# Last halves transposed on TensorE, a new tail of the joint stage, and two steps moved in loops

## What is computed

```python
# L0: two wide attentions (16 heads of 64), then a gated feed-forward
h = layer_norm(x, ln1_g, ln1_b); x = x + attention(h, h, Wq1, Wk1, Wv1, Wo1, bo1)
h = layer_norm(x, ln2_g, ln2_b); x = x + attention(h, ctx, Wq2, Wk2, Wv2, Wo2, bo2)
x = x + gated_feed_forward(layer_norm(x, ln3_g, ln3_b))
# L1: a narrow attention (16 heads of 8) on ctx, then norm and feed-forward
out = narrow_attention(x, ctx); out = out + feed_forward(layer_norm(out)); x = x + out
# L2: wide attention (16 heads of 64) of layer_norm(x) on ctx
x = x + wide_attention(layer_norm(x), ctx)
# L3: narrow attention (16 heads of 8) of x on ctx
x = x + narrow_attention(x, ctx)
```

## Time and profile before

| | us |
|---|---|
| median of 3 runs | 1729.83 (1729.8 to 1731.36) |
| the profiled execution | 1727.86 |
| its span, first to last instruction | 1726.1 |

### The profile page before, as it was taken

One profiled execution on the slowest core, in us unless ns is written; L12 is line 12 of the kernel. 1 busy time (PEld: TensorE's weight loads), 2 busy tenths in 40 slices (PEclk: granted clock), 3 DMA queues, 4 the chain that ended last, 5 costly groups with the idle time before them and its releaser, 6 DMA issues. The chain is left out here.

```text
span 1726.1 us, 48944 instructions
## 1 busy us (share of the span) xinstructions
PE 1638.1 (95%) x16520; PEld 1351.9 (78%) x16520; DVE 1310.8 (76%) x2408; ACT 1240.9 (72%) x3858; POOL 677.3 (39%) x946
## 2 busy tenths in 40 slices
PE   7999999999999999989899998988999999999997
PEld 6888888888888888779777777867787888787875
DVE  5777777777777777747688887656888888888885
ACT  5777777777777777623388886456888888888885
POOL 3444444454444444413222222643343434343431
PEclk9999999999999999989999999999999999999999
DMA  7776777777767767730000000014434344343441
GB/s 198 198 189 185 190 194 187 219 208 205 194 184 190 186 188 185 209 86 1 1 2 0 0 0 1 0 38 135 137 118 134 118 127 124 121 131 119 133 131 53
DMA packets 230743, 216.51 MB, mean 125 GB/s; under 512 B 19874, under 2 KB 228324, under 8 KB 230628
## 3 DMA queue, kind: packets, MB, share of 16 engines
q1 hardware_dynamic: 230628, 215.17, 45.2%
HBM read 112.34 MB, written 102.76 MB: 125 GB/s over the span
## 5 line engine op out<-in xcount | busy, mean ns | idle before, releaser
L658 ACT ACTIVATE L_probs<-L_scores,L_neg_max 128x128 f32<-128x128 f32 x512 | 182.7, 386 | 134.6 <-DVE L_neg_max L740 134.6
L854 POOL TENSOR_TENSOR L_probs<-L_probs,L_inv_sum 128x1024 f32<-128x1024 f32 x128 | 242.8, 1897 | 88.4 <-DVE L_inv_sum L760 88.4
L734 DVE TENSOR_REDUCE L_row_max<-L_scores 128x8 f32<-128x1024 f32 x128 | 156.1, 1219 | 41.5 <-PE L_scores L534 41.5
L1957 POOL TENSOR_TENSOR L2L_w_probs<-L2L_w_probs,L2L_w_inv_sum 128x1024 f32<-128x1024 f32 x64 | 121.4, 1897 | 129.7 <-DVE L2L_w_inv_sum L1783 129.5
L766 DVE STREAM_TRANSPOSE L_squares<-L_probs 128x1024 f32<-128x1024 f32 x128 | 156.6, 1223 | 0.3 <-POOL L_probs L854 0.3
L581 PE MATMUL L_ring<-L_probsT,L_v 128*64 128x128 f32 x2048 | 127.9, 277 | 9.5 <-issue 8.6
L581 PEld LDWEIGHTS L_ring<-L_probsT,L_v 128*64 128x64 f32 x2048 | 111.2, 137 | 29.9 <-issue 27.0
L534 PE MATMUL L_scores<-L_kT,L_qT 64*128 64x128 f32 x2048 | 131.8, 278 | 0.9 <-ACT L_kT L647 0.9
L534 PEld LDWEIGHTS L_scores<-L_kT,L_qT 64*128 64x128 f32 x2048 | 119.4, 188 | 12.5 <-ACT L_oT L647 8.1
L750 DVE TENSOR_REDUCE L_sums<-L_probs 128x8 f32<-128x1024 f32 x64 | 78.1, 1220 | 66.1 <-ACT L_probs L665 66.1
L1581 ACT ACTIVATE L2L_w_probs<-L2L_scores,L2L_w_neg_max 128x128 f32<-128x128 f32 x256 | 90.5, 372 | 39.3 <-DVE L2L_w_neg_max L1747 39.3
(11 more groups left out here) (220 smaller groups left out, 4617.0 us busy)
## 6 DMA issues: line engine op xcount, KB each, us to landing
L_relay<-L_squares SPq DMA_DIRECT2D x128, 512.0 KB, 3.4
L_probsT<-L_relay SPq DMA_DIRECT2D x512, 128.0 KB, 3.6
L2L_relay<-L2L_w_squares SPq DMA_DIRECT2D x64, 512.0 KB, 3.4
L2L_w_probsT<-L2L_relay SPq DMA_DIRECT2D x256, 128.0 KB, 2.9
out_x<-x SPq DMA_DIRECT2D x32, 64.0 KB, 2.7
L0a_wq<-in_L_xattn_Wq SPq DMA_DIRECT2D x2, 256.0 KB, 3.1
L0a_wk<-in_L_xattn_Wk SPq DMA_DIRECT2D x2, 256.0 KB, 3.7
L0a_wv<-in_L_xattn_Wv SPq DMA_DIRECT2D x1, 512.0 KB, 6.5
```

The costliest lines, as they stand in the source:

```text
L658: done = nc.scalar.activation(slot_probs(at, 0)[:, n, :], scores[:, 0, r, i, :], ACT.Exp, scale=layer_of(at).scale, bias=neg_max[:, n:n + ...
L734: nc.vector.tensor_reduce(row_max[:, s, :], slot(s), AX.X, ALU.max).then_inc(max_ready[s], 1)
L854: nc.gpsimd.tensor_tensor(to, to, inv_sum[:, :, s, :].unsqueeze(3) .to_broadcast([TOKENS, 2, GROUP, TOKENS]), ALU.mult).then_inc(divided, 1)
L1957: nc.gpsimd.tensor_tensor(to, to, w_inv_sum[:, :, s, :].unsqueeze(3) .to_broadcast([TOKENS, 2, GROUP, TOKENS]), ALU.mult).then_inc(w_divid ...
```

## The change

Four parts, all in the order of the work; the arithmetic is the same.

1. **L0's last halves.** The probabilities of (item, half) (62,1), (63,0) and (63,1) are transposed by TensorE (eight transpositions a half, two ring banks, one copied out by ScalarE and one by VectorE) and take no squares and no DMA. L3's weights are turned one step earlier. On SyncE's queue, from step 59 on, `back` of half 1 is issued before `away` of the next item's half 0.
2. **L1.** T0 (four heads) of t is transposed ahead of `score(t+1)`; T1 stays behind it.
3. **Joint stage, every step.** n.hT moves behind q1: TensorE does q1, n.hT, k1; ScalarE copies q1, n.hT, k1 behind the first four narrow exponentials, where n.hT had been ahead of them. The ring order is changed to match.
4. **Joint stage, end.** Item 31's halves are transposed by TensorE (16 transpositions, four copies by ScalarE) in a step of its own (31), in which `w_weigh(31)` and w.Wo(31) follow too; `tail_step` has them no more. For that, sums and division of item 31's half 1 are moved ahead into step 30: VectorE's `w_add_up(31)` stands before `n_row_maxima` there, and GpSimd's `w_divide(31, 1)` before `n_add_bias`.

```diff
@@ wide_attention
-    weights_step = items - 1
+    weights_step = items - 2
+    by_pe = ((items - 2, 1), (items - 1, 0), (items - 1, 1))
-    other_orders[weights_step] = [("weights", 0, "dve")] + order
+    other_orders[items - 3] = order[:9] + [("T2", 1, "dve"), ("T3", 1, "act")] + order[9:]
+    other_orders[items - 2] = order + [("T0", 1, "act"), ("T1", 1, "dve"), ("weights", 0, "dve")]
+    other_orders[items - 1] = order[:9] + [("T2", 0, "dve"), ("T3", 0, "act")] + order[9:]
@@ sync
-                if here(At(t), 1):
+                second = here(At(t), 1) and (t + 1, 1) not in by_pe
+                next_first = here(At(t), 2) and (t + 2, 0) not in by_pe
+                if second:
                     away(At(t + 1), 1)
-                if here(At(t), 2):
+                if second and t >= items - 5:
+                    back(At(t + 1), 1)
+                if next_first:
                     away(At(t + 2), 0)
...
@@ tensor
                 if here(t, 0):
                     weigh(t, 0)
+                    if t.n == items - 3 and t.i is None:
+                        transpose_probs(t.plus(1), 1)
+                    if t.n == items - 1:
+                        transpose_probs(t, 1)
                     weigh(t, 1)
+                if t.n == items - 2:
+                    transpose_probs(t.plus(1), 0)
+                    turn_weights(t)
...
@@ narrow_attention, tensor
             def step(t):
+                if here(t, 0):
+                    transpose_probs(t, 0)
                 if here(t, 1):
                     score(t.plus(1))
                 if here(t, 0):
-                    transpose_probs(t, 0)
                     transpose_probs(t, 1)
@@ wide_and_narrow
-             ("n.iT", -3, "act"), ("n.hT", -1, "act"), ("w.q1", 2, "act"), ("w.k1", 2, "act"), ("n.PV", -3, "dve"),
+             ("n.iT", -3, "act"), ("w.q1", 2, "act"), ("n.hT", -1, "act"), ("w.k1", 2, "act"), ("n.PV", -3, "dve"),
...
@@ tensor
+            def last_wide_step(t):
+                w_transpose_probs(t, 0)
+                w_weigh(t.plus(-1), 0)
+                w_weigh(t.plus(-1), 1)
+                w_transpose_probs(t, 1)
+                n_transpose_probs(t.plus(-3), 0)
+                n_transpose_probs(t.plus(-3), 1)
+                w_project_out(t.plus(-1))
+                n_score(t.plus(-2))
+                n_transpose_probs(t.plus(-3), 2)
+                n_transpose_probs(t.plus(-3), 3)
+                n_transpose_inverses(t.plus(-3))
+                w_weigh(t, 0)
+                w_weigh(t, 1)
+                n_transpose_h(t.plus(-1))
+                n_weigh(t.plus(-3))
+                n_queries_keys(t.plus(-1))
+                w_project_out(t)
+                n_project_out(t.plus(-3))
+                n_values(t.plus(-2))
+
...
+                if here(t, 2):
+                    w_queries(t.plus(2), 1)
                 if here(t, -1):
                     n_transpose_h(t.plus(-1))
                 if here(t, 2):
-                    w_queries_keys(t.plus(2), 1)
+                    w_keys(t.plus(2), 1)
...
@@ scalar
-                if here(t, -1):
-                    n_turned_h(t.plus(-1))
                 if here(t, -2):
                     n_exponentiate_0(t.plus(-2), 0)
                 if here(t, 2):
-                    w_projections(t.plus(2), 1)
+                    w_projection(t.plus(2), "w.q1", w_qT, 1)
+                if here(t, -1):
+                    n_turned_h(t.plus(-1))
+                if here(t, 2):
+                    w_projection(t.plus(2), "w.k1", w_kT, 1)
...
@@ vector
                 if here(t, -1):
                     w_finish(t.plus(-1))
+                if t.n + 1 == LAST_WIDE:
+                    w_add_up(t.plus(1))
+                    w_invert(t.plus(1), 1)
                 if here(t, -2):
                     n_row_maxima(t.plus(-2), 0)
                     n_negate_maxima(t.plus(-2))
...
@@ gpsimd
                 if here(t, -1):
                     n_copy_rows(t.plus(-1))
+                if t.n + 1 == LAST_WIDE:
+                    w_divide(t.plus(1), 1)
+                if here(t, -1):
                     n_add_bias(t.plus(-1))
```

More of the change, by code:

```diff
@@ L585, in weigh, with transpose_probs @@
                 filled_by(last, f"PV{s}")
+            def transpose_probs(at, s):
+                pe.wait_ge(divided, at.times(2, s + 1))
+                for n in (2 * s, 2 * s + 1):
+                    to = start_fill(f"T{n}", at)
+                    for i in range(GROUP):
+                        last = nc.tensor.transpose(to[:, TOKENS * i:TOKENS * (i + 1)],
+                                                   slot_probs(at, s)[:, GROUP * (n % 2) + i, :], ident[:, :])
+                    filled_by(last, f"T{n}")
             def transpose_h(at):
@@ L789, in turned_weights, with turned_probs @@
                 done.then_inc(emptied["dve"], 1)
+            def turned_probs(at, n):
+                await_filled(dve, f"T{n}", at)
+                nc.vector.tensor_copy(turned_to(at, n), by_head(bank(f"T{n}", at))).then_inc(emptied["dve"], 1)
             def step(t):
@@ L799, in step @@
                     subtract_maxima(t.plus(2))
-                if t.n == weights_step:
-                    turned_weights(t)
                 if here(t, -1):
                     finish(t.plus(-1))
-                if here(t, 1):
+                if t.n == items - 3 and t.i is None:
+                    turned_probs(t.plus(1), 2)
+                if t.n == items - 2:
+                    turned_probs(t.plus(1), 1)
+                    turned_weights(t)
+                if t.n == items - 1:
+                    turned_probs(t, 2)
+                if here(t, 1) and (t.i is not None or (t.n + 1, 1) not in by_pe):
                     turn_squares(t.plus(1), 1)
@@ L814, in step @@
                     invert(t.plus(2), 1)
+                if here(t, 2) and (t.i is not None or (t.n + 2, 0) not in by_pe):
                     turn_squares(t.plus(2), 0)
@@ L1226, in wide_and_narrow @@
     LANDED = 16 * SQUARES
-    ring = Ring(order, range(first, last + 1), BATCHES, {t: tail_order for t in range(BATCHES, last + 1)})
+    ring = Ring(order, range(first, last + 1), BATCHES,
+                {LAST_WIDE: last_wide_order, **{t: tail_order for t in range(BATCHES, last + 1)}})
     chunks = INNER // 128
@@ L1498, in n_project_out, with w_transpose_probs @@
                                            start=True, stop=True), "n.Wo")
+            def w_transpose_probs(at, s):
+                pe.wait_ge(w_divided[s], at.times(1, 1))
+                for n in (2 * s, 2 * s + 1):
+                    to = start_fill(f"w.T{n}", at)
+                    for i in range(GROUP):
+                        last = nc.tensor.transpose(to[:, TOKENS * i:TOKENS * (i + 1)],
+                                                   w_slot(at, s)[:, GROUP * (n % 2) + i, :], ident[:, :])
+                    filled_by(last, f"w.T{n}")
+            def last_wide_step(t):
[18 more added lines that the diff above has]
+                n_values(t.plus(-2))
             def tail_step(t):
@@ L1833, in n_finish, with last_wide_step @@
                                         ALU.add).then_inc(emptied["dve"], 1)
+            def last_wide_step(t):
+                n_add_up(t.plus(-3))
+                n_invert(t.plus(-3), 1)
+                n_repeat_inverses(t.plus(-3))
+                w_finish(t.plus(-1))
+                n_row_maxima(t.plus(-2), 0)
+                n_negate_maxima(t.plus(-2))
+                n_row_maxima(t.plus(-2), 1)
+                n_weighted(t.plus(-3))
+                n_subtract_maxima(t.plus(-2))
+                w_finish(t)
+                n_finish(t.plus(-3))
+                n_invert(t.plus(-2), 0)
             def tail_step(t):
@@ L1841, in tail_step @@
                     n_negate_maxima(t.plus(-2))
-                if here(t, -1):
-                    w_finish(t.plus(-1))
                 if here(t, -2):
@@ L1880, in step @@
                     n_negate_maxima(t.plus(-2))
-                if here(t, 1):
+                if here(t, 1) and t.n + 1 != LAST_WIDE:
                     w_turn_squares(t.plus(1), 0)
@@ L1960, in step @@
             def step(t):
-                if here(t, 0):
+                if here(t, 0) and t.n != LAST_WIDE:
                     w_divide(t, 1)
```

105 lines of the change are left out of this document (78 added, 27 removed).

## The result

| | before | after |
|---|---|---|
| median of 4 runs each, us | 1729.82 (1729.15 to 1731.36) | 1746.54 (1746.21 to 1747.27) |
| the profiled execution | 1727.86 | 1747.27 |
| its span | 1726.1 | 1745.2 |
| TensorE matmul, busy | 1638.1 (95%) | 1659.5 (95%) |

The account below looks back on a forecast made before the run. TensorE, busy 95% of the span, was taken as the bound, with holes differing by stage. The terms -8.5 - 12 - 11.5 + 2.5 = -29.5 took 1727.86 to 1698.4, median 1700 us, range 1692 to 1709.

Parts of the forecast that it names:

- The joint loop: Joint stage's steps: q1 ahead of n.hT covers TensorE's wait, 0.4 us a step; -11.5 us, bounds -5 and -14.1.
- The slower case: Rival, joint loop: n.hT's copy as late in every step as in step 30; about +40, 1751 us, chance 0.05.
- L0's end: End of L0: TensorE's waits for landing DMAs shrink, block ends 7.5 us earlier; -8.5 us, bounds -4 and -10.
- The 0.85 for the clock: Start of L0ff: if the clock stays up, the low-clock stretch shrinks by 1.7 us, of which half was taken.
- the rule weighed there: L0's tail: transposing doesn't count for the clock gate; as a rival, some 4.5 us less gain, 1705, chance 0.07.
- L1: L1 loop: T0 ahead of the score cuts each of 29 steps from 6.5 to 6.1 us; -12, bounds -6 and -14.
- The forecast's test: L1 loop: a stated sign that the prediction is wrong if the step stays above 6.3 us.
- Joint end: End of joint stage: narrow maxima and n.hT's copy come later in step 30; +2.5 us, bounds -3 and +6.
- The sum: Whole kernel: the four terms give -29.5 us, 1698.4 for the profiled execution and 1700 for the median.
- the one with the rivals: Whole kernel: range of 1690 to 1714 us with half-gain and clock cases inside, leaving out about 0.15.
- The half-gain rival: L1 and joint loops: a small late wait takes 0.2 us a step, 11 less gain, 1711, chance 0.17.

Follow-up runs that it names:

- e4: The kernel before with the third part alone (n.hT behind q1 in the joint stage's steps): 1721.43 us, ratio 0.9929.
- e12: The changed kernel without the 10 clock matmuls at the start of the joint stage: 1712.60 us, ratio 0.9891.
- e11: The kernel before with two steps a turn of the joint loop instead of four: 1725.96 us, ratio 0.9976.
- e3: The kernel before with the first part alone (L0's last halves transposed by TensorE): 1773.84 us, ratio 1.0235.
- e5: The changed kernel with two steps a turn of the joint loop instead of four: 1706.79 us, ratio 0.9854.
- e1: The changed kernel with 24 more clock matmuls at the start of the joint stage: 1718.44 us, ratio 0.9915.
- e10: The changed kernel without its fourth part, two steps a joint turn, L1's v copied before the subtraction, n.hT before exponentials in steps 30 and 31: 1702.58 us, ratio 0.9829.

## Why the prediction was wrong, point by point

- **The joint loop** (-11.5, measured +25.5) is the step that failed, and not in its working: the order gives -10.9 alone (e4), the wait before n.hT is gone from the loop and a plain step is 16.68, as said. What failed is the sum: it adds four terms, each worked out for its own stage, and puts at nothing, without a word, what a part in one stage does to the loop of another. The first part puts 54 TensorE instructions ahead of the joint loop (58 with part 3), and the stalls that follow cost 34.5 us in five turns (the ten steps at the turns take 209.1 us after and 174.6 in e12). No rival had it. The slower case that I gave (every step like step 30, 1751) came near the measured time by luck, with another mechanism. The profile's 49 packets were in front of me, and so were the 18.2 us of every fourth step, which by e11 is probably a fault of the same kind on a small scale.
- **L0's end** (-8.5, measured -5.9; 5.7 in e3): the order of the waits is as laid out, with 0.89 for ScalarE's copy as forecast. The landing of (61,1) came at 728.3 (1.1 of that from the run-in) instead of 725.5, and weigh(61) still waited 1.58. The 0.85 for the clock didn't come: L0ff still has a dip (0.62 granted in 752 to 756). It isn't the change that decides this: L0ff took 94.0 us instead of 95.65 in e5, which has the first part (1.00 granted in 752 to 756), and in e4, which hasn't. On the rule weighed there: the windows 720 to 744 show 1.00 with 24 transpositions among weigh and projections, so the trace gives no sign that these transpositions left the clock low here. With the same tail, e1 and e10 did run low behind the first eight transpositions and the wait of 2.0 to 2.3 us after them (0.50 granted in 732 to 736 of e10). The transpositions stood among matmuls and next to a wait, so the rule is neither borne out nor refuted.
- **L1** (-12, measured -5.4): the chain was laid out without the ring. That a fill waits for the copy of four places earlier stands in my own description of the kernel, and for T0 I didn't look up whose bank it takes. It is v's, whose copy stands behind the subtraction in VectorE's step: 0.1 a step. The other 0.12 a step is the loop's turn, 0.25 in every second step. The forecast's test, "wrong if L1's step stays above 6.3", named it.
- **Joint end** (+2.5, measured +4.4): `n_queries_keys` of step 30 is 2.6 later than before (1.9 forecast) and `n_score(30)` 6.9 later (6.5 forecast); `n_score(31)` is 3.5 later, not 2.1, by the lower clock among others (0.57 granted in 1717 to 1725). The lateness came as laid out; the size was short by 2, which is no more than the end of one kernel varies.
- **The sum**: without the stalls the changed kernel is 1.1% below the kernel before (e12), about 1711 on the median of before. So the four terms alone were 11 us too good, outside the forecast's own range (1692 to 1709) and inside the one with the rivals (to 1714): L1 6.6, L0 2.6, the end 1.9. The half-gain rival has just 1711, but by luck: it takes half of the gain from both loops, where the joint loop gave all of its own. The other 35 are the stalls.

## What to carry to other kernels

Before changing anything, read the number of instruction packets and the first step of every loop turn; if a long loop's body nearly fills what the engine seems to hold (here a body of 6.28 packets), any instruction added ahead of it, in any stage, can cost more than the change gives. Halve such a body, and pay 0.2 us a turn for it, rather than tune where it lies; and when a single edit is measured, see first whether the packets stayed the same. Where a fill is moved, look up whose bank it now waits for, and where that copy stands in its engine's step.

## What of the hardware was not expected

- TensorE with a body of 1607 instructions: no stall with 0, 4 or 18 instructions more ahead of it (49 packets), a stall at every turn with 54, 58 or 60 more (94 to 95 packets), none with 154 more (50). No run shows anything between "all stays" and "all is fetched again": 9 packets a turn, more than the 7 or 8 that the body touches.
- Such a stall shows as 3.9 us and 1.8 us of "issue" in TensorE's waits (up to 5.0 in e3), and costs 6.9 us in the new step order and 8.4 to 8.9 in the old one, partly by the lower clock behind it.
- With four steps a turn and no stall of TensorE, a turn's step was 1 to 2 us longer, with ScalarE (a body of 292 instructions) idle in it; two steps a turn took the q14 packets from 66 to 39 and all but 0.2 us of the loss away.
